# Moving the segment-maximum transfers from SyncE's to ScalarE's queue and waiting after every fourth record gather

## What is computed

```python
x = _layernorm(x + _L0_gnn_ref(x, edge_index, ...))   # 4-head attention over the edges of each source node
x = _layernorm(x + _L1_gnn_ref(x, node_vec1, ...))    # normalized neighbour sums
x = _layernorm(x + _L2_gnn_ref(x, edge_weight, edge_attr_3, ...))  # radial messages, summed by destination
x = _layernorm(x + _L3_gnn_ref(x, edge_index, ...))   # two graph convolutions

# in L0:
e = jax.nn.leaky_relu(a_src[:, src] + a_dst[:, dst] + fc_b[0], negative_slope=0.2)
seg_max = jax.ops.segment_max(e.T, src, num_segments=n)
e = jnp.exp(e - seg_max.T[:, src])
att = e / jax.ops.segment_sum(e.T, src, num_segments=n).T[:, src]
```

## Time and profile before

| | us |
|---|---|
| time, median of 3 runs | 20693.88 |
| profiled execution, span (its own time, nothing recorded around it) | 27567.4 |
| neighbour gathers on POOL, first to last, profiled | 1190.6 to 6047.6 |
| last sort ends, profiled | about 7582 |
| segment maximum, load to store, profiled | 7583.7 to 7836.3 |
| record gathers, profiled | 6066.6 to 6105.4 (32), 7854.8 to 11365.6 (2,528) |
| attention ends, profiled | about 13487 |
| last chunk row of L1 written, chunk gathers begin, profiled | 14278.8 |

### The profile page before, as it was taken

How to read it: one execution, slowest core, us unless ns; L and a number is a source line. 1 busy time by engine, 2 the same in 40 slices (tenths; PEclk the granted TensorE clock), 3 DMA queues, 4 the chain that set the end, 5 groups by cost and what they waited for, 6 DMA issues and landing times.

```text
span 27567.4 us, 293981 instructions
## 1 busy us (share of the span) xinstructions
PE 10462.8 (38%) x63545; PEld 7879.1 (29%) x63546; DVE 17275.5 (63%) x25284; ACT 5969.5 (22%) x13901; POOL 13400.7 (49%) x14067
## 2 busy tenths in 40 slices
PE   0040000000110000377642377766666777523522
PEld 0030000000100000366532244444444444422421
DVE  9897474559930000488775577777777778554555
ACT  0002121113300000122220033333333334400500
POOL 0287676650047777300016566666656664164065
PEclk6555555555555555688755577777777777555555
DMA  1133434430000000011252300000000002623623
GB/s 13 35 24 28 29 30 29 30 23 0 1 25 7 8 7 8 18 30 30 76 191 69 57 10 10 10 10 10 10 9 9 10 10 32 215 65 52 232 65 62
DMA packets 1751559, 1096.00 MB, mean 40 GB/s; under 512 B 1217323, under 2 KB 1658124, under 8 KB 1750028
## 3 DMA queue, kind: packets, MB, share of 16 engines
q0 software_dynamic: 454272, 412.11, 12.0%
q1 hardware_dynamic: 1089820, 431.09, 6.5%
q10 hardware_dynamic: 207344, 251.51, 2.9%
HBM read 700.94 MB, written 391.12 MB: 40 GB/s over the span
## 4 chain that ended last, share of the span: by engine, by line
DVE 30%; another core or an unknown queue 24%; DVEq 16%; issue 15%; PE 10%; ACT 2%; DMA 2%; ACTq 1%; POOL 0%; SPq 0%; POOLq 0%
DVEq L2477 5%; DVE arena L1750 4%; DVE arena L1749 4%; PE banks L1405 3%; DVE arena L2173 3%; DVE srcs L2472 3%; DVEq L2167 2%; PE banks L1347 2%; DVE hot L2162 2%; DVE arena L1722 2%; DVEq L2205 2%; DVE red L2478 2%; DVEq L495 1%; DVE arena L1567 1%
## 5 line engine op out<-in xcount | busy, mean ns | idle before, releaser
L807 POOL DMA_INDIRECT srcs<-spread,nbx x2808 | 2653.0, 945 | 5878.9 <-issue 3638.9
L785 POOL DMA_INDIRECT gat<-tab,nbr x3328 | 3449.9, 1037 | 2544.7 <-issue 1304.1
L1405 PE MATMUL banks<-w2rows,dsts 128*128 128x384 f32 x6656 | 3538.6, 673 | 1156.9 <-DVE srcs L2472 799.6
L751 POOL DMA_INDIRECT pay<-records,nbr x2560 | 2710.6, 1059 | 2606.5 <-DMA nbr<-ids_dst 1766.6
L785 POOL DMA_INDIRECT gat<-tab,pay x3328 | 3173.5, 954 | 1080.1 <-issue 890.9
L1193 PE MATMUL banks<-ident,arena 128*128 128x128 f32 x2240 | 439.6, 383 | 5795.5 <-DVE arena L1750 2139.5
L2478 DVE TENSOR_REDUCE red<-srcs 128x80 f32<-128x1280 f32 x1664 | 2473.9, 1487 | 151.6
L2173 DVE TENSOR_TENSOR arena<-arena,banks 128x96 f32 (+2 forms) x4472 | 1207.7, 270 | 2141.5 <-remote 969.1
L912 ACT COPY banks<-arena 128x1024 f32<-128x1024 f32 (+1 forms) x1508 | 1325.0, 880 | 4899.7 <-issue 1445.8
L1264 PE MATMUL banks<-srcs,hot 128*128 128x96 bf16 (+1 forms) x11232 | 1169.0, 280 | 3128.0 <-DVE hot L2162 1971.2
L2467 DVE TENSOR_TENSOR srcs<-banks,g_s 128x512 f32<-128x512 f32 x1664 | 1139.3, 685 | 1571.8 <-remote 1145.0
(11 more groups left out here) (394 smaller groups left out, 21816.3 us busy)
## 6 DMA issues: line engine op xcount, KB each, us to landing
spread<-srcs SPq DMA_DIRECT2D x936, 192.0 KB, 2.8
dsts<-key_rows SPq DMA_DIRECT2D x234, 512.0 KB, 4.0
spread<-srcs ACTq DMA_DIRECT2D x468, 204.0 KB, 2.4
staged<-gat SPq DMA_DIRECT2D x416, 148.0 KB
gat<-staged ACTq DMA_DIRECT2D x416, 148.0 KB
dsts<-key_rows ACTq DMA_DIRECT2D x117, 512.0 KB, 4.2
gat<-tab,nbr POOLq DMA_INDIRECT x3328
gat<-tab,pay POOLq DMA_INDIRECT x3328
```

The lines of the kernel that those rows point to most:

```text
L751: pool.indirect_dma_start(out=pay[:, s, t, :], out_offset=None, in_=records, in_offset=bass.IndirectOffsetOnAxis(ap=nbr[:, s, t:t + 1], ax ...
L785: pool.indirect_dma_start(out=gatv(s, GC[pas])[:, t, :], out_offset=None, in_=TAB[pas], in_offset=bass.IndirectOffsetOnAxis(ap=row, axis=0 ...
L807: pool.indirect_dma_start(out=chunk_rows(s, c)[:, q, :], out_offset=None, in_=rows, in_offset=bass.IndirectOffsetOnAxis(ap=nbx[:, r, s * X ...
L1405: last = t_.matmul(bank[1 + 2 * (p % 2) + h][:, 0:384], hid_rows[:, s % 2, 2 * p + h, :], w2rows[:, :], start=True, stop=True)
```

## The change

Two things in three places. ACT, when its part of the sorts is done, now waits for the last stores of `adst_tiles` and issues the load and the store of the segment-maximum table; SP's program no longer has them, so that `record_loads` follows round 0 at once. And POOL waits, after every fourth record gather (BURST = 4), until all gathers of that slot so far have landed.

```diff
+BURST = 4
@@ SP
             sp.wait_ge(ids_sent, 16)
-            for s in range(SLOTS):
-                sp.wait_ge(adst_out[s], 16 * ITERS)
             record_round(0, True, False)
-            sp.wait_ge(row_keys_made, 3)
-            sp.dma_start(arena[:, 0:NT * HEADS], adst_tiles).then_inc(seg_loaded, 16)
-            sp.wait_ge(seg_done, 1)
-            sp.dma_start(max_tiles, arena[:, 0:NT * HEADS]).then_inc(seg_stored, 16)
             record_loads()
@@ POOL, collect()
                             ).then_inc(rec_in[s], 16)
+                            if t % BURST == BURST - 1:
+                                pool.wait_ge(rec_in[s], i * (16 * TPS) + 16 * (t + 1))
+                                pool.nop(nofuse=True)
@@ ACT
                 sort_operands(chunkA, chunkB, LOGC)
+            for s in range(SLOTS):
+                act.wait_ge(adst_out[s], 16 * ITERS)
+            act.wait_ge(row_keys_made, 3)
+            act.dma_start(arena[:, 0:NT * HEADS], adst_tiles).then_inc(seg_loaded, 16)
+            act.wait_ge(seg_done, 1)
+            act.dma_start(max_tiles, arena[:, 0:NT * HEADS]).then_inc(seg_stored, 16)
             for s in range(SLOTS):
                 act.wait_ge(staged_out[s], 16 * ITERS)
             act.wait_ge(seg_stored, 16)
```

## The result

The kernel takes 21,653.56 us with the change (median of four runs, 21,648.15 to 21,669.05) and 20,702.39 us without it (four runs, 20,691.62 to 20,712.36): a ratio of 1.0456, with a 95% interval of 1.0444 to 1.0469. It is slower by 951 us. Slower was forecast, but by 340 us, and the range ended at 21,370.

What follows compares the result with a forecast made beforehand. Bound by two chains ending within 40 us, spread (9410) and POOL's record gathers (9449). Starting at 5629, 640 runs of 6.5 us end at 9789, 340 us later: 20,694 + 340 = 21,034, rounded 21,030; range 20,240 to 21,370.

Steps and rivals of the forecast that it cites:

- The tie: Beside gathers PE advances one instruction per gather, DVE waits; 4,834 of the profiled execution's 6,873 extra us, taken as profile-only.
- Two chains end close together: Before the chunk gathers, DVE's chain through attention and spread (9410) and POOL's record gathers (9449) end within 40 us.
- The rebuilt order: Timed run's order of events without the tie: sorts end 6016, attention 8618, spread 9410, POOL's record gathers 9449.
- 1.25 us per gather: POOL's period for a record gather without waits: 0.94 us plus a gap of 0.30, so 2,528 take 3160 us.
- The move costs nothing on ACT's queue: Two big transfers issued from ACT after the last sort: cost 0, or 0.7 us if not hidden.
- the term of the runs: Four record gathers with POOL's wait take 6.5 us (6.2 to 7.0) instead of 5.0; 640 runs take 4,160 us.
- the page price: Skill page's 2.0 us per DMA plus bytes: 2.01 us instead of 2.46, 290 us less over 640 runs.
- Hidden: Rival: at 1.16 us or less per gather, record gathers end before the spread; no change, 20,694 +-30; chance 0.26.
- the closing sum: Check on 20,694: from POOL's 9449, later stages leave 5,430 us for radial against 5,617; collects can give up to 730.
- Tie, faster: Rival: tie partly real in timed runs, pauses free PE; gains 50 to 830, middle 450, giving 20,240; chance 0.30.
- The port: Rival: gathers beside L2221 and L2162 take 1.79 us, not 0.94; waits absorb up to 350 us; 20,840; chance 0.06.
- The signs by which I would be wrong: Run of four under 6.0 us; delaying or shortening timed record gathers doesn't move the time; timed run much faster.

## Why the prediction was wrong in size and right in kind

**What held.** *The tie is not in timed runs.* The kernel before, profiled again, has none of it, and the stretch of 6,873 us belonged to that one execution. *Two chains end close together.* The rebuilt order said 9410 for the spread and 9449 for POOL; the trace says 9413 and 9498. That the first is met to 3 us is in part luck: the attention begins 35 us earlier than rebuilt (6253 instead of 6288), and its projection, norms and spread take longer than 792. *1.25 us per gather* is real and not the recording (1.249 in a profile whose span is that of a timed run). *The move costs nothing on ACT's queue, the waits more than the early start gives.* Each is shown by a run of its own (the move alone, the waits alone). The forecast was that the chunk gathers move as a block with POOL's end: they move by 942, the time by 951.

**What failed is the term of the runs,** "3 x 1.25 + 2.46 + (0 to 0.78)", taken as 6.5 with a high end of 7.0. It was 7.36, in two parts.

- *POOL's wake-up.* The landing was right: SP's store comes 2.48 us after the last gather's start (6981.42 to 6983.90), against the 2.46 predicted. POOL goes on 0.67 us after SP (6984.57), not the 0.29 that the 6.5 implied. A quiet run is 3 x 1.25 + 3.15 = 6.90. So POOL's 3.15 us from the last gather's start to its next one is a sum of the landing and its own start, and only the second was undersized. Outside the spread 552 runs took 3,905 us, 7.07 each. (The rest above 6.90 is about what the last section finds by the iteration, 1 us over eight runs.) The chunk gather's 0.78 was the nearest row, and its whole should have been taken, not a point between it and nothing. Against 6.5 that is 552 x 0.57 = 315 us.
- *The runs beside the spread.* I priced all 640 runs by a quiet place. From 8600 to 9405, with DMA queues moving 201 GB/s, 352 gathers are 88 runs of 805/88 = 9.15 us: 88 x 2.65 = 233 us. The row was there: the profile before showed 59% DMA share and 201 GB/s in the spread, and the prediction even had the record gathers run beside it, yet took no other price. Two things grow there against the attention: the pause, from a mean of 2.30 us (leaving out one of 11.82) to one of 3.74 (88 pauses, 2.01 to 5.98), and the gathers themselves, from a busy time of 0.94 us each to 1.11. The second comes without waits too: in the kernel before, 575 gathers take 805 us there, some 87 more than at 1.249. Here is one of the longer pauses:

```profile
9009.25 0.94 POOL L746 DMA_INDIRECT pay<-records,nbr  x1 [0.30 <-issue]
9015.18 0.94 POOL L746 DMA_INDIRECT pay<-records,nbr  x1 [4.98 <-DMA pay<-records,nbr]
```

**Smaller terms.** The neighbour gathers end at 5712, not 5610, so the start is 100 us later: my own rows gave 5642 by their mean duration (0.976 us), I took less, and the mean period from 2075 on was 1.302. The kernel before ends its gathers 49 us later than predicted (it starts them 35 us earlier, at 6254, and needs 3,244 us instead of 3,160, nearly all of it beside the spread), which takes 49 off the difference. In all 340 + 315 + 233 + 100 - 49 = 939, of the 942 us by which the chunk gathers moved.

**What the page price would have given.** By the estimate from the Trainium skill's page "DMA: Bandwidth & Descriptors", section on the anatomy of a GpSimd DMA, this gather takes 2.01 us, and the change would have cost 50 us. The trace has 2.48 us to SP's next instruction, 3.15 to POOL's, and more under load. Both hold an engine's own start behind the landing, so they don't refute 2.01 us for the DMA alone, but they are what a wait costs; the measurements decide.

**The rivals.** *Hidden* asked for a gather of 1.16 us or less; it is 1.25. What the prediction held against it, the closing sum, could not have told: with 1.16 the spread (9410) would have ended last instead of POOL (9449), 39 us apart, and the sum had up to 730 us to give. *Tie, faster* fell with the second profile of the kernel before: pauses set nothing free. In the same 2,346 us of the attention PE executes 13,280 matmuls beside uninterrupted gathers and 13,309 beside gathers with pauses. (The "some 44 steps" of the stretched stage are 40 by the earlier trace rows; the loss is then 22 us larger, and nothing hangs on it.) *The port* rested on a row that was misread. The two 1.79 us gathers of the earlier trace rows run from 8713.31 to 8717.20 and don't lie beside L2221 or L2162 at all: DVE stands idle from 8714.25 to 8778.13, and the gather in progress when L2221 begins takes 1.09 us (kernel before, stretched execution):

```profile
8777.71 1.09 POOL L751 DMA_INDIRECT pay<-records,nbr  x1 [0.30 <-issue]
8778.13 1.25 DVE L2221 TENSOR_TENSOR msg<-gat,banks 128x1056 f32<-128x1056 f32 x1 [63.88 <-issue]
```

Of the 153 record gathers of that stretch that last 1.6 to 1.95 us, 30 overlap an L2221 or an L2162, and 123 neither. What lengthens them was not found. Beside the attention 1,879 gathers are busy for 1,773.34 us in the unstretched execution, 0.944 each, so there is nothing to earn. The lock on a shared port pair that the Trainium skill describes ("SBUF — State Buffer", "Who interferes with whom") shows no effect in that row. Nor should it: that section of the Trainium skill holds a VectorE instruction with at most one input in SBUF, outside the 2-port modes, to be free of it, and L2221 and L2162 each read one of their two inputs from `banks`, which is PSUM.

**The range.** It took the bounds of the run's price at one place as bounds for all places, and no case held a longer landing. The signs by which I would be wrong named only a run under 6.0 us; the miss was on the other side. The profile of the changed kernel was expected to be stretched too, at 24,000 to 26,500 us; it was 21,651.

## What to carry to other kernels

Price a wait for a DMA by the consumer's own restart (here 3.15 us from the last gather's start, not the 2.46 after which another engine goes on), and once per stage: the same wait is dearer where other queues are loaded. Before adding waits to a stream of small gathers, find where the chain that it belongs to meets the others; here 414 us of slack, 2% of the time, were less than what 160 such waits took (474 us), while 638 waits for an older landing were free. And where a profile's span is a third over the timed runs, take a second profile before any term is read from it.

## What the runs showed of the hardware that was not expected

- **One profiled execution was stretched by a third, and only one.** In it PE advanced by about one instruction per gather; none of the nine later profiles, each of one execution, shows it, the second of the same kernel among them, though back-to-back neighbour gathers run beside the sorts in every one. What set it off stays open.
- **A gather's landing depends on what the other queues move.** The mean pause behind a run of the changed kernel is 2.30 us in the attention (35 GB/s, the 11.82 below left out), 3.74 beside the spread (201 GB/s), and 2.22 again after it (4 GB/s). The two longest are 15.00 us, after the issue of the load of the segment-maximum table, and 11.82 us, after that of its store. SP, which waits for the same gathers, goes on as late as POOL does, so it is the landing that is late:

```profile
5986.41 0.35 ACTq L955 DMA_DIRECT2D arena<-adst_tiles  x1
...
6005.68 0.35 SPq L590 DMA_DIRECT2D by_dst<-pay  x1
6006.35 0.94 POOL L746 DMA_INDIRECT pay<-records,nbr  x1 [15.00 <-DMA pay<-records,nbr]
...
6239.47 0.34 ACTq L957 DMA_DIRECT2D max_tiles<-arena  x1
...
6258.30 0.94 POOL L746 DMA_INDIRECT pay<-records,nbr  x1 [11.82 <-DMA pay<-records,nbr]
```

- **The price of a wait does not grow with the run before it, though the quotients say so.** Divided by the number of waits, the loss beside the attention is 1.96, 2.06 and 2.18 us for runs of two, four and eight, and 2.39 for sixteen, where 1,678 gathers, with 105 waits among them, were done in the time of 1,879 (201 x 1.249 / 105):

```profile
6254.00:8600.00 2346.00, 1583.32 (x1678) 0.89 0.19 35
```

  The pauses themselves do not differ. Leaving out the first gather of each iteration of 32, they are 2.20, 2.23, 2.25 and 2.21 us on the mean, for runs of two, four, eight and sixteen. What differs is how many waits share two losses that come by the iteration, however many waits it has: the pause ahead of its first gather is some 0.5 us longer (2.70 to 2.75), and in one iteration of three there is a gap of some 1.9 us in the middle of a run, ahead of the second gather of the third slot (0.5 us per iteration on the mean). Here are both in the changed kernel:

```profile
6941.79 0.94 POOL L746 DMA_INDIRECT pay<-records,nbr  x1 [2.62 <-issue]
...
6972.08 0.94 POOL L746 DMA_INDIRECT pay<-records,nbr  x1 [1.86 <-issue]
```

  That is about 1 us per iteration over 16, 8, 4 or 2 waits, which leaves about 1.9 us for a wait in each version. In the kernels whose waits expose nothing, or that have none, both are missing (between 6254 and 8600 all gaps there are 0.30 to 0.32, but for the 6.83 shown above). What causes them was not tested.
- **Gathers without waits feel the same load far less.** Beside the spread they come every 1.40 us (805/575) instead of 1.25, because they are busy for 1.10 us instead of 0.94; their gaps stay at 0.30. A gather with its share of a wait went from 1.76 us (2346/1330) to 2.29 (805/352) between the same two stretches.
